# Row 9 of the third product summed inside the second sweep, beside diagonal tiles of units that are still held

## The reference

```python
# layer 0
e = concat(par_u0*par_u1*(diag_u*x_u @ W_u) + x_u, par_i0*par_i1*(diag_i*x_i @ W_i) + x_i)
h = adj @ (adj.T @ e)
x = layernorm(x + layernorm(h)*gamma + beta + x)
# layer 1: Chebyshev, K = 4
T0 = x
T1 = adj @ T0
T2 = 2*(adj @ T1) - T0
T3 = 2*(adj @ T2) - T1
out = layernorm(x + T0 @ w[0] + T1 @ w[1] + T2 @ w[2] + T3 @ w[3] + bias)
```

## Time and profile before

| | us |
|---|---|
| median of 3 runs | 1214.84 |
| lowest, highest of them | 1209.78, 1215.15 |
| the profiled execution's own time | 1212.09 |
| its span in the profile | 1210.2 |

### The profile page before, as it was taken

How to read it: one execution, slowest core, us unless ns; L and a number is a source line. 1 busy time by engine, 2 the same in 40 slices (tenths; PEclk the granted TensorE clock), 3 DMA queues, 4 the chain that set the end, 5 groups by cost and what they waited for, 6 DMA issues and landing times.

```text
span 1210.2 us, 13868 instructions
## 1 busy us (share of the span) xinstructions
PE 1109.8 (92%) x5004; PEld 479.3 (40%) x5004; DVE 922.2 (76%) x960; ACT 332.1 (27%) x594; POOL 257.6 (21%) x420
## 2 busy tenths in 40 slices
PE   4999999999999997899889999999999999598794
PEld 3454445444444453444233333344344443122231
DVE  2698798999899898697777766665666667588783
ACT  1456456456466465300000000000100000011010
POOL 0476655464363453100000000000000000011111
PEclk9999999999999999899999999999999999798898
DMA  7999999999999987899999999999999999999991
GB/s 227 300 289 298 282 299 315 289 296 279 299 275 282 296 233 167 186 313 286 266 347 347 336 313 293 318 292 255 261 336 319 336 304 330 348 306 342 353 352 30
DMA packets 372730, 350.82 MB, mean 290 GB/s; under 512 B 11612, under 2 KB 371332, under 8 KB 372692
## 3 DMA queue, kind: packets, MB, share of 16 engines
q1 hardware_dynamic: 259092, 237.35, 70.5%
q10 hardware_dynamic: 110880, 110.11, 31.8%
q0 software_dynamic: 2720, 2.86, 0.9%
HBM read 348.97 MB, written 1.31 MB: 289 GB/s over the span
## 4 chain that ended last, share of the span: by engine, by line
PE 55%; SPq 12%; DVE 12%; ACT 10%; ACTq 5%; issue 4%; POOL 1%; DMA 1%; DVEq 0%; POOLq 0%
PE bank L1174 31%; ACT terms L774 9%; SPq L337 7%; ACTq L279 5%; SPq L326 4%; DVE turned L496 4%; PE bank L1225 4%; PE bank L1187 3%; PE bank L1044 2%; PE bank L1004 2%; PE bank L1032 2%; PE bank L1056 2%; PE bank L1016 2%; DVE shared L516 2%; PE bank L1203 1%
## 5 line engine op out<-in xcount | busy, mean ns | idle before, releaser
L1174 PE MATMUL bank<-turned,terms 128*128 128x512 f32 x680 | 301.4, 596 | 4.5 <-DVE turned L496 3.1
L386 POOL COPY raw<-raw 32x512 f32<-32x512 f32 x320 | 194.8, 609 | 243.6 <-DVE raw L533 205.1
L516 DVE STREAM_TRANSPOSE shared<-shared 32x512 f32<-32x512 f32 x320 | 224.0, 700 | 4.1
L1004 PE MATMUL bank<-shared 128*64 128x256 f32 x1600 | 206.1, 385 | 6.5 <-DMA shared<-in_adj 6.4
L496 DVE STREAM_TRANSPOSE turned<-raw 128x2048 f32<-128x2048 f32 x72 | 165.1, 2301 | 58.9 <-PE bank L1174 50.0
L496 DVE STREAM_TRANSPOSE turned<-shared 128x2048 f32<-128x2048 f32 x68 | 156.0, 2302 | 60.3 <-PE bank L1174 46.0
L774 ACT COPY terms<-terms 32x512 f32<-32x512 f32 x320 | 197.1, 616 | 5.1 <-DVE terms L526 0.9
L1174 PEld LDWEIGHTS bank<-turned,terms 128*128 128x128 f32 x680 | 126.6, 190 | 170.3 <-issue 164.0
L431 POOL DMA_DIRECT2D out<-scratch x40 | 21.7, 549 | 681.1 <-DVE scratch L724 681.0
L1004 PEld LDWEIGHTS bank<-shared 128*64 128x64 f32 x1600 | 111.6, 136 | 88.4 <-issue 33.1
L765 ACT COPY scratch<-bank 128x512 f32<-128x512 f32 x80 | 46.6, 585 | 131.2 <-PE bank L1016 130.9
(11 more groups left out here) (144 smaller groups left out, 1059.7 us busy)
## 6 DMA issues: line engine op xcount, KB each, us to landing
shared<-in_adj SPq DMA_DIRECT2D x100, 1024.0 KB, 10.7
raw<-in_adj SPq DMA_DIRECT2D x106, 512.0 KB, 10.6
raw<-in_adj ACTq DMA_DIRECT2D x106, 512.0 KB, 12.3
shared<-in_adj SPq DMA_DIRECT2D x104, 512.0 KB, 10.6
shared<-in_adj ACTq DMA_DIRECT2D x104, 512.0 KB, 12.1
raw<-in_adj SPq DMA_DIRECT2D x80, 256.0 KB, 7.6
xq<-in_x POOLq DMA_DIRECT2D x40, 32.0 KB, 6.2
out<-scratch POOLq DMA_DIRECT2D x40, 32.0 KB, 5.2
```

The costliest lines, as they stand in the source:

```text
L386: last = nc.gpsimd.tensor_copy(moved[Q32 * c:Q32 * (c + 1), :, :, Q32 * q:Q32 * (q + 1)], beside[Q32 * q:Q32 * (q + 1), :, c, :, :])
L516: last = nc.vector.transpose(low_turned[Q32 * c:Q32 * (c + 1), :, :, Q32 * q:Q32 * (q + 1)], low[Q32 * q:Q32 * (q + 1), :, :, Q32 * c:Q32 ...
L1004: last = nc.tensor.matmul(t_bank[H * odd:H * (odd + 1), 0:PW], e[:, s * SB + b, :], panels[slot][:, s * SB + b, :], start=(k == 0 and b < ...
L1174: last = nc.tensor.matmul(sum_bank[parity][:, :], terms[:, c * GB + i, columns], turned[place][:, i * BANK:(i + 1) * BANK], start=(first a ...
```

## The change

The order of the last two sweeps is written out as one list, `late`, of entries (UP, g, c), (DIAG, g, g) and (LOW, g, c). The UP entries are sweep 2's tiles in their old order. After the first unit of the row that follows an even row g (8, 6, 4, 2), three entries come in between: the diagonal tile (g, g) of T3, whose unit has been held in its slot since row g, and two tiles of row 9, (9, g + 1) and (9, g).

- The new function `add_diag_and_low` multiplies (g, g) and (9, g + 1) side by side: the first into the upper half of row g's bank, which still holds T3's sum of row g, the second into the lower half of bank 0, in which row 9 sums up throughout. (9, g) follows with `add_tile_halves`.
- On ScalarE, `take_up` copies a row's sums as `take_row` did, but for rows 8, 6, 4 and 2 the T2 half alone; `take_late_diag` copies the T3 half after the diagonal tile. TensorE's first tile of the next row with the same bank waits for it (`late_diag_kept`).
- `write_r` is done after four tiles of the next row or just ahead of the first tile that needs it.
- The rest of the third sweep has 43 tiles, in the order of rows 7, 0, 9, 8, 1, 6, 2, 5, 4, 3 (row 0, one tile from a unit held since sweep 2, in the midst of row 7; the ten outputs in the order 0, 7, 9, 8, 1, 6, 2, 5, 4, 3). Rows alternate between banks 6 and 7.
- A tile that is in a unit still held is no longer loaded again. The list gives 25 units for UP, 4 for row 9 in between, and 21 after it: 50 in place of 55.

```diff
-        sweep2 = [(g, c) for g in DOWN for c in range(NG - 1, g, -1)]
-        ROWS3 = [g for k in range(NG // 2) for g in (NG - 1 - k, k)]
+        ROWS3 = [0, 7, 9, 8, 1, 6, 2, 5, 4, 3]
+        LOW_BANK = {0: 6, 7: 7, 9: 0, 8: 6, 1: 7, 6: 6, 2: 7, 5: 6, 4: 7, 3: 6}
+        for g in ROWS2_ORDER:
+            for window in range(NG // SPAN - 1, (g + 1) // SPAN - 1, -1):
+                late += [(UP, g, c) for c in (SPAN * window + 1, SPAN * window) if c > g]
+                if open_diag is not None:
+                    late += [(DIAG, open_diag, open_diag), (LOW, NG - 1, open_diag + 1), (LOW, NG - 1, open_diag)]
+                    open_diag = None
+            if g % SPAN == 0 and g > 0:
+                open_diag = g
...
+        write_at = [min(up_end[i] + 4, needed[i]) for i in range(NG - 1)]
...
+            u = held.get(key) if n >= NG * NG else len(loads) - 1
+            if loads and u is not None and loads[u][0:2] == key and (n > NG * NG or u == len(loads) - 1):
+                loads[u] = (*key, n)
...
+            def take_up(i, g):
+                n, part = ROWS1 + i, slice(0, H) if g in DIAGS else slice(0, P)
+                load_through(row_end[n] - T1)
+                act.wait_ge(tile_used, TURNED + row_end[n])
...
+            def take_late_diag(n, g):
+                load_through(NG * NG + n + 1)
+                act.wait_ge(tile_used, TURNED + T2 + n + 1)
...
+            def add_diag_and_low(t, places, g, parity, c, bank, first, middle=None):
+                pe.wait_ge(tile_turned, t + 2 + RAW)
+                for i in range(GB):
+                    diag_tile = nc.tensor.matmul(sum_bank[parity][H:P, :], terms[:, g * GB + i, 2 * H:3 * H],
...
+                    low_tile = nc.tensor.matmul(bank[0:H, :], terms[:, c * GB + i, 2 * H:3 * H],
...
+                if kind == UP:
+                    elif c == NG - 1 and g + 2 in DIAGS:
+                        pe.wait_ge(late_diag_kept, DIAGS.index(g + 2) + 1)
```

More of the change, by code:

```diff
@@ L206, in resnorm_chebyshev @@
         row_kept = sem("row_kept")
+        late_diag_kept = sem("late_diag_kept")
         row_back = sem("row_back")
@@ L228, in resnorm_chebyshev @@
         assert TILED == RAW and TILED == NS - 3 and TILED * GB == 2 * ITEMS and ITEMS % AT == 0
-        sweep2 = [(g, c) for g in DOWN for c in range(NG - 1, g, -1)]
-        ROWS3 = [g for k in range(NG // 2) for g in (NG - 1 - k, k)]
-        sweep3 = [(g, c) for g in ROWS3 for c in range(g, -1, -1)]
+        assert NG == 10 and SPAN == 2
         FINISH = 4
-        END3 = [sum(g + 1 for g in ROWS3[:i + 1]) for i in range(NG)]
         PAIR = 2 * NG
+        ROWS2_ORDER = DOWN[1:]
+        ROWS3 = [0, 7, 9, 8, 1, 6, 2, 5, 4, 3]
@@ new lines, in resnorm_chebyshev @@
+        for pair in LAST_LOW:
+            late += [(LOW, pair[0], SPAN * pair[1] + 1), (LOW, pair[0], SPAN * pair[1])] if pair else [(LOW, 0, 0)]
+        late_tiles = [(g, c) for _, g, c in late]
+        up_end = [max(n for n, (kind, row, _) in enumerate(late) if kind == UP and row == g) for g in ROWS2_ORDER]
+        low_start = [min(n for n, (kind, row, _) in enumerate(late) if kind == LOW and row == g) for g in ROWS3]
+        low_end = [max(n for n, (kind, row, _) in enumerate(late) if kind == LOW and row == g) for g in ROWS3]
@@ L239, in resnorm_chebyshev @@
+        assert low_end == sorted(low_end) and len(late) == NG * NG
+        DIAGS = [g for kind, g, _ in late if kind == DIAG]
+        needed = [min(n for n, (kind, row, c) in enumerate(late) if c == g and n > up_end[i])
+                  for i, g in enumerate(ROWS2_ORDER)]
+        write_at = [min(up_end[i] + 4, needed[i]) for i in range(NG - 1)]
         first_rows = [(g, DOWN[k + i]) for k in range(0, NG, 2) for g in range(2) for i in range(2)]
         T2 = T1 + NG * NG
-        late_tiles = sweep2 + sweep3
@@ L243, in resnorm_chebyshev @@
         row_end = {n: T1 + ((n + 1) * NG if n else PAIR - 2) for n in range(NG)}
         ROWS1, ROWS2 = NG, 2 * NG - 1
-        for n in range(ROWS1, ROWS2 + NG):
-            row_end[n] = row_end[n - 1] + (n - ROWS1 + 1 if n < ROWS2 else ROWS3[n - ROWS2] + 1)
+        for i in range(NG - 1):
+            row_end[ROWS1 + i] = T2 + up_end[i] + 1
+        for j in range(NG):
+            row_end[ROWS2 + j] = T2 + low_end[j] + 1
         def place1(g, c, n):
@@ L262, in resnorm_chebyshev @@
         load_of = []
+        held = {}
         for n, (g, c) in enumerate(all_tiles):
-            if loads and loads[-1][0:2] == (g, c // SPAN):
-                loads[-1] = (g, c // SPAN, n)
-            else:
-                loads.append((g, c // SPAN, n))
-            load_of.append(len(loads) - 1)
+            key = (g, c // SPAN)
+            u = held.get(key) if n >= NG * NG else len(loads) - 1
+            if loads and u is not None and loads[u][0:2] == key and (n > NG * NG or u == len(loads) - 1):
+                loads[u] = (*key, n)
+            else:
+                loads.append((*key, n))
+                u = len(loads) - 1
+            if n >= NG * NG:
+                held[key] = u
+            load_of.append(u)
+        assert all(load_of[n] < SLOTS or loads[load_of[n] - SLOTS][2] < n for n in range(len(all_tiles)))
         def free_after(u):
@@ L724, in finish @@
                 nc.vector.tensor_tensor(y, y, inverse_root(GB), ALU.mult).then_inc(out_made, 1)
[L727 to L739, removed]
-                late_tile(n)
[L741 to L746, removed]
+            for n in range(len(late)):
+                late_tile(n)
+                if n == TURNED - 1:
+                    write_q(NG - 1)
+                if n == TURNED:
+                    write_u(NG - 1)
+                for i, g in enumerate(ROWS2_ORDER):
+                    if write_at[i] == n:
+                        write_r(ROWS1 + i, g)
+                if n - 1 - FINISH in low_end:
+                    finish(low_end.index(n - 1 - FINISH))
+            for j in range(NG):
+                if low_end[j] + 1 + FINISH >= len(late):
+                    finish(j)
         @block.scalar
@@ L926, in _ @@
             take_u(NG - 1, 1)
-            for i, g in enumerate(DOWN[1:]):
-                take_row(ROWS1 + i, i % 2, sums2[:, g * BANK:(g + 1) * BANK])
             def take_p(i):
@@ L936, in take_output @@
                 nc.scalar.activation(o_turned, o_bank[:, :], ACT.Identity, bias=bias_column[:, :]).then_inc(o_copied, 1)
[L938 to L949, removed]
+            for n, (kind, g, c) in enumerate(late):
+                if n - 1 in low_end:
+                    load_through(NG * NG + n + 1)
+                    take_p(low_end.index(n - 1))
+                    take_output(low_end.index(n - 1))
+                if n == len(late) - 2:
+                    take_p(NG - 1)
+                if n in up_end:
+                    take_up(up_end.index(n), g)
+                if kind == DIAG:
+                    take_late_diag(n, g)
+                if n in low_end:
+                    take_low(low_end.index(n))
+                if n - 3 in low_end:
+                    j = low_end.index(n - 3)
+                    load_through(NG * NG + low_end[j] + 1 + FINISH)
                     root(2 * NS + j, GB)
-                take_row(ROWS2 + i, (ROWS2 + i) % 2, None)
             take_output(NG - 1)
@@ L1178, in add_tile, with add_tile_halves @@
                 last.then_inc(tile_used, 1)
-            def add_tile_halves(t, place, c, parity, first, last_tile, middle=None):
+            def add_tile_halves(t, place, c, bank, first, last_tile, middle=None, odd_first=False):
                 pe.wait_ge(tile_turned, t + 1 + RAW)
@@ L1294, in _ @@
             turn_u(NG - 1)
[L1295 to L1304, removed]
             def turn_p(i, g):
+                if i == 0:
+                    pe.wait_ge(row_copied, ROWS2 + 1)
                 for c in range(GB):
@@ L1316, in output_sums @@
                 pe.wait_ge(row_kept, 2 * NG + NG - 1)
+                pe.wait_ge(late_diag_kept, len(DIAGS))
                 if i:
@@ L1340, in turn_output @@
                 last.then_inc(out_summed, 1)
[L1342 to L1363, removed]
@@ new lines, in between @@
+            def between(n):
+                if n - 1 in up_end:
+                    i = up_end.index(n - 1)
+                    turn_row(ROWS1 + i, i % 2, H)
+                if n - 1 in low_end:
+                    turn_p(low_end.index(n - 1), ROWS3[low_end.index(n - 1)])
+                if n == len(late) - 2:
+                    turn_p(NG - 1, ROWS3[-1])
+                if n == len(late) - 1:
+                    output_sums(NG - 1, ROWS3[-1])
+                    output_p(NG - 1, ROWS3[-1])
@@ new lines, in _ @@
+            for n, (kind, g, c) in enumerate(late):
+                t, place = T2 + n, late_place(n)[0]
+                middle = lambda: between(n)
+                if kind == UP:
+                    i = ROWS2_ORDER.index(g)
+                    if i == 0:
```

(28 more changed lines are left out.)

36 lines of the change are left out of this document (28 added, 8 removed).

## The result

The changed kernel takes 1196.82 us in the median of four runs (1196.05 to 1198.46), where the kernel before took 1214.07 in four (1209.78 to 1215.15). The ratio is 0.9864, with a 95% interval of 0.9841 to 0.9887: 1.1 to 1.6% faster. The forecast was 1197. The span of the profiled execution is 1195.1 us, 15.1 less than before.

The account below looks back on a forecast made before the run. TensorE was taken to bound sweep 2 and the DMA, narrowly, the third sweep; -26.0 + 1 + 5 + 2 = -18 us from 1212.1 gave 1194.1, as a median 1197, range 1184 to 1211.

Parts of the forecast that it names:

- (a): Sweep 2: four groups of moved tiles lengthen TensorE's work by 21.2 us, plus 1 us for tiling switches.
- (b): Third sweep: twelve transpositions leave VectorE, -26.3 us; in sweep 2 they are hidden behind TensorE.
- (c): Third sweep: VectorE's waits for units to land go, at most all 20.9 us.
- (d): Third sweep: DMA and VectorE chains are level and at times wait for each other, +5 us given back.
- (e): Sweep 2: TensorE stalls after the held unit lets the load queues run dry, +2 us, bounds 0 and 5.
- The rest after the last transposition: End of the kernel: 21.8 us of outputs and stores, which the change does not shorten.
- The gain in full: Rival: the end follows the DMA, so the saved loads gain 30 us, 1184 us; chance 0.15.
- TensorE taking over: Rival: in the third sweep TensorE at a lower clock sets the time, 1205 to 1212 us; chance 0.18.
- ScalarE's issues ahead of its copies: Rival: sweep 2 copies wait behind load issues, 6.1 us each; six make it slower, 1234 us; chance 0.10.
- The loads were saved: Denies the rival that units are still loaded twice, 55 as before, above 1214 us; chance 0.02.

Follow-up runs that it names:

- the run with half of the bytes: Kernel before with half of each of its last 30 units loaded: 1184.66 us; the changed kernel with its last 21 so loaded: 1189.22 us.
- The run with 51 units: Changed kernel with the unit of tile (8, 8) alone loaded again instead of held: 1197.6 us, ratio 0.9876.
- the split `finish`: Changed kernel with finish cut in two, the instructions behind ScalarE's square root coming two tiles later: 1189.68 us, ratio 0.9812.

## Why the prediction was right

**What bounds the stages.** Right for sweep 2. For the third sweep, "set by the DMA, but not by much" was right, but the reading of how much was not: VectorE's 20.9 us of waits were taken for all that the units cost, and the run with half of the bytes shows 28 us. I read the rest as ScalarE's held-up issues, which reach VectorE as waits for square roots and output rows; TensorE's higher clock in that run may have a part in it. The 6.1 and 10.5 us of waits for output rows and square roots were in the trace, under other releasers, and the sum took them as fixed.

**(a) Sweep 2 longer:** +21.2 and 1 for switches; measured +22.7 in all, 5.4 us for a group, 0.1 above what the prediction gave as the limit. Right in kind, and nearly in size.

**(b), (c) and (d), the third sweep:** -26.3 - 20.9 + 5 = -42.2; measured -41.8. One wait of 3.7 us is left where 5 us were given back. The sum is right; its parts are less clean than it looks. VectorE's busy time fell by 27.4 us where 26.3 were counted, and other waits, taken as fixed, changed too (for output rows 6.1 to 5.2 us, for square roots 10.5 to 12.9, and 2.5 for the turning of a row). That the two chains are level, as (d) had it, is borne out: cheaper units gave 6.8 us, a shorter chain of VectorE 6.3.

**(e) The stall after the hold:** +2; measured nothing. The fifth unit was issued at 863.66, near the 863.3 worked out. It landed by 873.3, some 2.6 us before the 875.9 that were estimated, and TensorE came to its first tile only at 879.04, not at 877.4, and went on without a gap. The run with 51 units confirms that the empty queues cost nothing.

**The rest after the last transposition** was taken as unchanged, 21.8 us. This is the step that failed: it is 25.5, +3.7. Before, VectorE waited for its last units and TensorE was caught up; now no unit is waited for at the end, and TensorE still has work in hand when the last tile is turned. TensorE is busy 9.6 us in that stretch, where it was 6.0 in the earlier trace rows. The second half of the last tile, from the chain that ended last, before and after:

```profile
1191.66 1.03 PE bank L1187 x4
```

```profile
1176.48 1.03 PE bank L1232 x4
```

That is 3.3 us after the last transposition before and 6.9 after the change. The run of the kernel before with half of the bytes has 24.7 for the rest, with the old order, so most of the increase comes without the new order.

Of the forecast -18 us, sweep 2 was 1.5 us better (22.7 for 24.2 with the stall), the third sweep 0.4 worse, the start 0.3 and the end 3.7: -15.1 in the profiled spans. The medians differ by 17.3, so that 1197 was met so closely is partly chance.

**The rivals.** The gain in full did not come: even with half of the bytes the changed kernel gives 1189. TensorE taking over: the granted clock was 0.95 in the third sweep, above the 0.91 before, so the feared fall did not come; that TensorE is close behind VectorE is shown by the split `finish`. ScalarE's issues ahead of its copies: it happened once in sweep 2, for 0.58 us, where that rival needed four or more at 6.1 each. The loads were saved, 100 units.

## What to carry to other kernels

Price a saved load by what the next engine leaves of it, stage by stage: here five loads of 6.0 us gave 15 us, and without them the same order of work gained nothing at all. When an engine that copies results also issues loads, a full queue shows up as waits for that engine, under names that have nothing of a DMA; count them when you ask what the loads cost. Two chains that are strung together both show up when you make either longer or shorter, so one such run doesn't name the one that sets the time. Where a stage stops waiting at its end, look at the engine behind: its backlog becomes the tail.

## What the runs showed of the hardware

An issue of loads on ScalarE's queue is not a fixed cost: two transfers took 0.92 us at 863.66, when the queues stood empty, and 5.86 us at 898.33, when four earlier ones of ScalarE had not landed yet, and the copy behind them started only when they were issued. Two queues with work moved 339 to 349 GB/s together, one alone 209 (where first one queue's packets move and then the other's). I had not expected that queues standing empty for 12 us in a stage with 100% TensorE and a DMA demand of 322 GB/s would cost nothing; four units at hand were enough.
